# Feed-forward of a decoder layer: second products of three shared pieces behind the experts, two row and result buffers, early low parts on GpSimd

## The reference

```python
router = xf @ gate_w.T
probs = softmax(router)                        # 8 experts
top_p, top_i = top_k(probs, 2)
h = silu(xf @ expert_fc1[e].T) * (xf @ expert_fc2[e].T)       # 352 wide
out_e = h @ expert_proj[e].T                   # weighted by top_p, summed over 2 experts
s = silu(xf @ shared_fc1.T) * (xf @ shared_fc2.T)             # 1408 wide
out = x + experts + sigmoid(xf @ shared_gate_w.T) * (s @ shared_proj.T)
```

## Time and profile before

| what | us |
|---|---|
| three timed runs | 1404.07, 1404.05, 1395.89 (median 1404.05) |
| profiled execution | 1395.68 |
| its span, first to last instruction | 1393.9 |
| shared stage, from the router's first product to the last first product | 722.5 to 1085.2 |
| experts, to their last product | 1085.2 to 1354.7 |
| tail | 1354.7 to 1393.9 |

### The profile page before, as it was taken

One profiled execution on the slowest core, in us unless ns is written; L12 is line 12 of the kernel. 1 busy time (PEld: TensorE's weight loads), 2 busy tenths in 40 slices (PEclk: granted clock), 3 DMA queues, 4 the chain that ended last, 5 costly groups with the idle time before them and its releaser, 6 DMA issues. The chain is left out here.

```text
span 1393.9 us, 24148 instructions
## 1 busy us (share of the span) xinstructions
PE 1325.5 (95%) x8442; PEld 1069.3 (77%) x8442; DVE 849.8 (61%) x1516; ACT 486.1 (35%) x764; POOL 511.6 (37%) x365
## 2 busy tenths in 40 slices
PE   7999999998799999999889999999999999999995
PEld 5777778876567777777558888888878889999984
DVE  5766666787788888888644665555571242222237
ACT  4222222234366666566655111111110233323220
POOL 1122222134543434343240028421160675564055
PEclk9999999999899999999999999999999999999997
DMA  7992000003755554557200003230001434443257
GB/s 256 322 324 103 0 0 0 0 9 102 196 168 152 160 170 142 152 147 202 62 24 0 24 31 149 103 115 23 24 23 31 187 128 144 151 150 132 76 167 241
DMA packets 85035, 159.83 MB, mean 115 GB/s; under 512 B 8576, under 2 KB 61952, under 8 KB 81536
## 3 DMA queue, kind: packets, MB, share of 16 engines
q1 hardware_dynamic: 78688, 124.19, 28.4%
q0 software_dynamic: 6272, 34.61, 6.9%
HBM read 109.22 MB, written 69.47 MB: 128 GB/s over the span
## 5 line engine op out<-in xcount | busy, mean ns | idle before, releaser
L1526 ACT ACTIVATE b_pf<-b_rt,b_zero 128x1024 f32<-128x1024 f32 x128 | 142.7, 1115 | 118.6 <-PE b_rt L1197 118.2
L1366 DVE TENSOR_REDUCE b_mx<-b_rt 128x4 f32<-128x1024 f32 x128 | 156.3, 1221 | 36.0 <-PE b_rt L1185 35.4
L2064 DVE SCALAR_TENSOR_TENSOR residual<-c_yp,c_shared,residual 128x512 f32<-128x512 f32 x144 | 103.8, 744 | 114.7 <-PE c_yp L43 114.7
L41 PE MATMUL c_fc<-c_xh,c_w 128*128 128x512 f32 x352 | 137.8, 392 | 0.0
L43 PE MATMUL c_fc<-c_xh,c_w 128*128 128x512 f32 x352 | 137.2, 390 | 0.0
L42 PE MATMUL c_fc<-c_xl,c_w 128*128 128x512 f32 x352 | 137.1, 390 | 0.0
L2217 ACT ACTIVATE c_s<-c_fc 128x512 f32<-128x512 f32 x44 | 26.3, 598 | 231.8 <-PE c_fc L43 231.7
L41 PE MATMUL c_fc<-c_ring,c_xTl 128*128 x312 | 105.6, 338 | 0.0
L42 PE MATMUL c_fc<-c_ring,c_xTh 128*128 x312 | 101.1, 324 | 0.0
L43 PE MATMUL c_fc<-c_ring,c_xTh 128*128 x312 | 101.0, 324 | 0.0
L1879 POOL TENSOR_TENSOR c_w<-c_wraw,c_zero 128x1536 fp32r<-128x1536 f32 x9 | 24.7, 2749 | 202.4 <-DMA c_wraw<-in_c_ws 108.4
(11 more groups left out here) (404 smaller groups left out, 3495.1 us busy)
## 6 DMA issues: line engine op xcount, KB each, us to landing
weights_b<-b_pack SPq DMA_DIRECT2D x128, 200.0 KB
c_eraw<-in_c_we POOLq DMA_DIRECT2D x8, 2176.0 KB, 9.4
b_pack<-b_hi SPq DMA_DIRECT2D x56, 256.0 KB, 2.5
c_rows_in<-in_b_ctx SPq DMA_DIRECT2D x39, 256.0 KB, 9.6
c_rows_out<-in_b_ctx SPq DMA_DIRECT2D x39, 256.0 KB, 9.8
c_xe<-c_rows_in SPq DMA_DIRECT2D x39, 256.0 KB, 3.2
c_rows_out<-c_ye SPq DMA_DIRECT2D x39, 256.0 KB, 2.1
c_wraw<-in_c_ws SPq DMA_DIRECT2D x11, 768.0 KB, 4.2
```

Source lines behind the costliest of these rows:

```text
L41: nc.tensor.matmul(out, ll, rh, start=start, stop=False)
L1366: nc.vector.tensor_reduce(out=mx[:, :, 2 * p:2 * p + 2].rearrange("p t e -> p e t"), in_=rt[:, 0:2, :].rearrange("p e (t s) -> p e t s", s ...
L1526: nc.scalar.activation(pf[:, s:s + 2, :], rt[:, 2:4, :], ACT.Exp, scale=XD ** -0.5, bias=zero[:, :]).then_inc(e_done, 1)
L2064: nc.vector.scalar_tensor_tensor(out=X[:, t, :], in0=yp[:, (n * 4 + k) % 3, :], scalar=shared[:, t:t + 1], in1=X[:, t, :], op0=ALU.mult, o ...
```

## The change

NOW becomes 32: pieces 8, 9 and 10 are held (HELD = 3), so 12 blocks p wait for their second products, and `held_down` sums three pieces per group. The raw rows of the three pieces lie in `keep`, `wraw[2]` and `wraw[0]`, their low parts in `keep_low`, `w[2]` and `w[0]`. FIXED = 5 high parts have a place at once: four in `w[1]`, the fifth in a new tile `fifth`; the other seven reuse the five places, each behind the products that read it, and are all made in the tail. `xe` shrinks to two buffers and moves to memory that the router used, `ye` shrinks to two, `se` loses its unused columns. SP loads tile n + 4 where it loaded n + 6, and no longer waits for the shared stage's end before the first loads. ACT makes the five high parts in tiles 2 to 6; the five low parts to them are made by Pool, between its fetch and its split of expert 3. The other seven are DVE's, in a new hand-written order of the tail: there the early sums of group 3 and its late sums come before its shared sums, which finish that group, while in groups 0 to 2 the late sums do. The gate of the early gathers becomes `done + 2`.

```diff
     LAG = 2
-    NOW = STEPS - 2 * G
+    HELD = 3
+    NOW = STEPS - HELD * G
+    FIXED = 5
...
-        with ExitStack() as view:
-            xe = sb("xe", [P, 4, C], FP32, view)
...
-        se = sb("se", [P, 2, 512])
+        se = sb("se", [P, 2, 384])
         hTh, hTl = sb("hTh", [P, 2, 384], FP32R), sb("hTl", [P, 2, 384], FP32R)
-        ye = sb("ye", [P, 3, C])
+        ye = sb("ye", [P, 2, C])
+        fifth = sb("fifth", [P, C], FP32R)
+        sb("beside", [P, C // 2])
...
+        with ExitStack() as view:
+            xe = sb("xe", [P, 2, C], FP32, view)
...
         def held_raw(n):
 
-            g, second = (n - NOW) % G, (n - NOW) // G
-            return wraw[0][:, g // 2, g % 2 * C:(g % 2 + 1) * C] if second else keep[:, g, :]
+            g, f = (n - NOW) % G, n // G
+            return keep[:, g, :] if f == HID - 3 else wraw[(f + 2) % 3][:, g // 2, g % 2 * C:(g % 2 + 1) * C]
 
         def held_low(n):
-            g, second = (n - NOW) % G, (n - NOW) // G
-            return w[0][:, g // 2, g % 2 * C:(g % 2 + 1) * C] if second else keep_low[:, g, :]
+            g, f = (n - NOW) % G, n // G
+            return keep_low[:, g, :] if f == HID - 3 else w[(f + 2) % 3][:, g // 2, g % 2 * C:(g % 2 + 1) * C]
 
         def held_high(p):
 
-            if 4 <= p < 6:
-                return w[2][:, 1, C * (p - 3):C * (p - 2)]
-            return w[1][:, p % 6 // 2, p % 2 * C:(p % 2 + 1) * C]
+            u = p % FIXED
+            return fifth[:, :] if u == 4 else w[1][:, u // 2, u % 2 * C:(u % 2 + 1) * C]
 
         def pair(p):
-            return NOW + p % 2 * G + p // 2
+            return NOW + p % HELD * G + p // HELD
...
             def load(n):
-                if n >= 4:
-                    sp.wait_ge(te_done, n - 3)
-                sp.dma_start(rows_at(n), rows_in[n * P:(n + 1) * P, :]).then_inc(xe_in[n % 4], 16)
+                if n >= 2:
+                    sp.wait_ge(te_done, n - 1)
+                sp.dma_start(rows_at(n), rows_in[n * P:(n + 1) * P, :]).then_inc(xe_in[n % 2], 16)
 
             piece(2)
             for f in range(3, HID):
                 piece(f)
             sp.wait_ge(scattered, 16 * 2 * NT)
-            sp.wait_ge(ymm_done, 4 * G * 9)
-            for n in range(6):
+            for n in range(4):
                 load(n)
             for n in range(SLOTS):
                 sp.wait_ge(ye_done, n + 1)
-                sp.dma_start(rows_out[n * P:(n + 1) * P, :], ye[:, n % 3, :]).then_inc(ye_out[n % 3], 16)
-                if n + 6 < SLOTS:
-                    load(n + 6)
+                sp.dma_start(rows_out[n * P:(n + 1) * P, :], ye[:, n % 2, :]).then_inc(ye_out[n % 2], 16)
+                if n + 4 < SLOTS:
+                    load(n + 4)
...
+                if e == RING:
+                    for p in range(FIXED):
+                        pool.wait_ge(ph_done, p + 1)
+                        nc.gpsimd.tensor_tensor(held_low(pair(p)), held_raw(pair(p)), as_f32(held_high(p)), ALU.subtract).then_inc(pool_low, 1)
                 expert(e)
             done = pool.value_load(plan[0:1, E - 2:E - 1], min_val=1, max_val=SLOTS)
-            pool.wait_ge(ye_done, done + 3)
+            pool.wait_ge(ye_done, done + 2)
...
-                if 2 <= n < 8:
-                    pair_low(n - 2)
-            def expert_sum(t, k):
-                if k:
-                    dve.wait_ge(landed1[t // 4], 64)
-                    dve.wait_ge(dadded, t + 1)
+            def early_sums(a, b):
+                for t in range(a, b):
+                    dve.wait_ge(landed0[t % 3], 16 * (t // 3 + 1))
+                    nc.vector.scalar_tensor_tensor(out=X[:, t, :], in0=early[:, t, :], scalar=gain[:, 0, t:t + 1],
+                                                   in1=X[:, t, :], op0=ALU.mult, op1=ALU.add).then_inc(summed, 1)
+
+            def early_summed(t):
+                if t < POOLED:
+                    dve.wait_ge(pooled, t + 1)
                 else:
-                    dve.wait_ge(landed0[t % 3], 16 * (t // 3 + 1))
-                nc.vector.scalar_tensor_tensor(out=X[:, t, :], in0=(early, late)[k][:, t, :], scalar=gain[:, k, t:t + 1],
-                                               in1=X[:, t, :], op0=ALU.mult, op1=ALU.add).then_inc(finished if k else summed, 1)
+                    dve.wait_ge(summed, t + 1 - POOLED)
+
+            def late_sums(g):
+                for t in range(4 * g, 4 * g + 4):
+                    dve.wait_ge(landed1[g], 64)
+                    if g < G - 1:
+                        dve.wait_ge(dadded, t + 1)
+                    else:
+                        early_summed(t)
+                    nc.vector.scalar_tensor_tensor(out=X[:, t, :], in0=late[:, t, :], scalar=gain[:, 1, t:t + 1],
+                                                   in1=X[:, t, :], op0=ALU.mult, op1=ALU.add).then_inc(finished if g < G - 1 else joined, 1)
 
             def held_sums(g):
                 for k in range(4):
                     t = 4 * g + k
                     dve.wait_ge(dm_done, t + 1)
-                    if t < POOLED:
-                        dve.wait_ge(pooled, t + 1)
+                    if g < G - 1:
+                        early_summed(t)
                     else:
-                        dve.wait_ge(summed, t + 1 - POOLED)
+                        dve.wait_ge(joined, k + 1)
                     nc.vector.scalar_tensor_tensor(out=X[:, t, :], in0=sum_at(g, k), scalar=shared[:, t:t + 1],
-                                                   in1=X[:, t, :], op0=ALU.mult, op1=ALU.add).then_inc(dadded, 1)
-
-            def expert_sums(a, b, k):
-                for t in range(a, b):
-                    expert_sum(t, k)
-
-            expert_sums(POOLED, 9, 0)
+                                                   in1=X[:, t, :], op0=ALU.mult, op1=ALU.add).then_inc(dadded if g < G - 1 else finished, 1)
+
+            early_sums(POOLED, 9)
+            pair_low(5)
+            early_sums(9, 12)
+            pair_low(6)
             held_sums(0)
-            pair_low(6)
             pair_low(7)
-            expert_sums(9, 12, 0)
+            early_sums(12, 16)
+            pair_low(8)
+            late_sums(0)
             held_sums(1)
-            expert_sums(0, 4, 1)
-            expert_sums(12, 14, 0)
+            pair_low(9)
+            pair_low(10)
+            late_sums(1)
+            pair_low(11)
             held_sums(2)
-            expert_sums(4, 8, 1)
-            expert_sums(14, 16, 0)
+            late_sums(2)
+            late_sums(3)
             held_sums(3)
-            expert_sums(8, 16, 1)
...
             def pair_high(p):
                 if p == 0:
                     act.wait_ge(ymm_done, 4 * NOW)
-                if p == 6:
-                    act.wait_ge(pm_done, 1)
-                if p == 7:
-                    act.wait_ge(dm_done, 4)
+                if p >= FIXED:
+                    g, j = (p - FIXED) // HELD, (p - FIXED) % HELD
+                    if j == HELD - 1:
+                        act.wait_ge(dm_done, 4 * g + 4)
+                    else:
+                        act.wait_ge(pm_done, (HELD - 1) * g + j + 1)
                 nc.scalar.copy(held_high(p), held_raw(pair(p))).then_inc(ph_done, 1)
...
-                if 2 <= n < 8:
+                if 2 <= n < 2 + FIXED:
                     pair_high(n - 2)
-            for k in range(3):
-                act.wait_ge(ye_out[k], 16 * ((SLOTS + 2 - k) // 3))
-            act.sem_inc(ye_done, 3)
-            pair_high(6)
-            pair_high(7)
+            for k in range(2):
+                act.wait_ge(ye_out[k], 16 * ((SLOTS + 1 - k) // 2))
+            act.sem_inc(ye_done, 2)
+            for p in range(FIXED, HELD * G):
+                pair_high(p)
 
...
-                for j in range(2):
-                    p = 2 * g + j
-                    pe.wait_ge(pl_done, p + 1)
+                for j in range(HELD):
+                    p = HELD * g + j
+                    if p < FIXED:
+                        pe.wait_ge(pool_low, p + 1)
+                    else:
+                        pe.wait_ge(pl_done, p - FIXED + 1)
+                    k_w = (HID - HELD + j) % 3
                     for k in range(4):
                         a = slice(k * P, (k + 1) * P)
                         last = matmul3(nc, sum_at(g, k), (held_high(p)[:, a], held_low(pair(p))[:, a]),
-                                       (w[j][:, 0, 2 * C:PW], w[j][:, 1, 2 * C:PW]), j == 0, j == 1)
-                        if j == 1:
+                                       (w[k_w][:, 0, 2 * C:PW], w[k_w][:, 1, 2 * C:PW]), j == 0, j == HELD - 1)
+                        if j == HELD - 1:
                             last.then_inc(dm_done, 1)
-                    if j == 0:
+                    if j < HELD - 1:
                         last.then_inc(pm_done, 1)
...
```

(10 more changed lines are left out.)

7 lines of the change are left out of this document (4 added, 3 removed).

## The result

| what | before | after |
|---|---|---|
| median of 6 timed runs, us | 1402.87 (1395.89 to 1404.07) | 1384.13 (1382.6 to 1385.96) |
| profiled execution | 1395.68 | 1384.43 |
| its span | 1393.9 | 1382.6 |
| router's first product at | 722.5 | 724.7 |
| shared stage, from there to its last first product | 362.4 | 350.2 |

The changed kernel is faster by 1.3%: ratio of the timed runs 0.9873, 95% interval 0.9853 to 0.9894. The forecast was 1383.3 us. The medians are 18.7 us apart, the two profiled executions only 11.3 in span. The profile of before was taken in one of its fastest executions (1395.68, where six runs lie between 1395.89 and 1404.07), the profile of after near its median. So the stages are compared in the profiles, and the kernels by the timed runs.

The account below looks back on a forecast made before the run. PE was taken to bound the shared stage and experts, a relay of ACT, Pool and DVE the tail. 12.2 + 3.7 + 0.9 - 0.3 = 16.5 us takes 1395.68 to 1379.2; plus 4.1 gives 1383.3, range 1375 to 1394.

Parts of the forecast that it names:

- step 1: Shared stage: piece 8's 48 second products leave (10.9 us) and a long DVE low part vanishes (1.3): 12.2 us gained.
- step 2: Experts' first tiles: low parts leave DVE, five going to Pool, so none stalls beside a long Pool instruction: 3.7 us gained.
- step 3: Experts' row loads: two buffers instead of four leave 0.1 us margin in the tightest places: 0.3 us lost, at most 9.5.
- step 4: Tail behind the experts: late gathers start 4.0 us earlier, added PE and DVE work fits, DVE ends 0.9 us earlier.
- rows late: Rival, experts: three loads sent with expert weights land late, half clock behind each, 9.5 us back, 1388.7 us; chance 0.17.
- Gathers and sums in each other's way: Rival, tail: five added DVE low parts push Pool's indirect gathers, 3.7 us back, 1382.9 us (middle 1387.0); chance 0.08.
- The gain is not made: Rival, tail: it grows by what the 48 moved matmuls save, PE's groups strung out; 1391 to 1396 us; chance 0.12.
- Slower: Rival, experts: every row load comes late and stretches each tile; 1413 us at landings of 11.7 us; chance 0.05.
- a tail longer by more than 3 us: Sign of a wrong prediction: time from the experts' last product to the end grows by more than 3 us.
- PE's waits in the experts above 4 us: Sign of a wrong prediction: PE's waits in the experts exceed 4 us.

Follow-up runs that it names:

- a0: The changed kernel unaltered, measured again in the first group: median 1385.77 us, ratio 0.9901 to the kernel before.
- f3: The changed kernel unaltered, measured again in the last group: median 1387.66 us, ratio 0.9869 to the kernel before.
- f1: The changed kernel with row loads ahead of the store's wait, two early gathers in flight, no early sums on Pool: 1380.77 us, 0.9825 of the kernel before.
- f2: The changed kernel with row loads ahead of the store's wait, two early gathers in flight, one early sum on Pool: 1384.76 us, 0.9859 of the kernel before.
- b0: The changed kernel with two held pieces instead of three, all else as changed: 1396.97 us, 0.9973 of the kernel before.

## Why the prediction held, and where it missed

The forecast of 16.5 us against the profiles, term by term. The slow tiles are counted against 6.73 us, tile 37 against the 6.27 that it took before.

| term | said | measured |
|---|---|---|
| step 1, shared stage | 12.2 | 12.2 |
| step 2, low parts off the first tiles | 3.7 | 3.7 |
| step 3, late rows | -0.3 | -2.6 |
| last tiles beside the gathers | not foreseen | -1.6 |
| step 4, tail | 0.9 | 1.8 |
| all that runs ahead of the feed-forward | 0 | -2.2 |
| sum, in span | 16.5 | 11.3 |

**Step 1** was right to a tenth: 48 products at 0.227 us and the one long low part. PE was busy 266.02 of 267 us there, so what left it could shorten the stage by its full length. Taking it back alone returned 362.6.

**Step 2** was right: tiles 3 and 4 took 9.48 + 7.65 us before, 3.7 more than two usual ones, and 6.7 each after. Returning the low parts to DVE cost 3.6 at tile 3. The reason given, a low part that stands still while a long Pool instruction runs, is shown four times, by 6.43 and 4.56 us before, 6.57 with two pieces held and 4.47 with the low parts on DVE. By the rule of the Trainium skill (SBUF — State Buffer, "Who interferes with whom"), a DVE instruction with two SBUF inputs contends with a GpSimd one that reads SBUF, for a pair of ports that one of them locks; the traces agree, the DVE one ending 0.5 to 0.6 us after Pool's each time.

**Step 3** had the right mechanism and a price too small by 2.3 us. The price was read from landings of 9.6 beside 9.8 us, margin 0.1, and set at 0.3 us; the loads took 10.65 and 11.29 us and cost 0.96 and 1.68 us at tiles 11 and 16 (7.69 and 8.41 for 6.73). The error is the assumption that the landing of a transfer stays as it was when the kernel around it changes. The bound held: the prediction's 9.5 us (its 3 x 3.1 is 9.3) is far above 2.6, and no low clock followed these waits (granted clock 1.00 from 1160 to 1170 and from 1196 to 1206). The fetch after these two cost nothing: SP's load was issued 0.08 us ahead of it (1213.21 and 1213.29), not behind it. The rival *rows late* happened in two of three places, at 2.6 us instead of 9.5.

**The last tiles** were no step. The working treated the early gathers as work of Pool, hidden by PE, and gave the experts' body as full up to 1324; from 1332 on the gathers ran, and that stretch was not read for what stands beside them. In the one profile of before nothing was slow there, so the view could not have given the size; c0, the kernel before with two row buffers, shows 2.7 us at tile 36 and 5.3 at tile 37 with the old work around it. So this loss can come without the held piece and the earlier gate. It differs from kernel to kernel and from execution to execution, 0.4 to 8.8 us, and is a part of why runs of one kernel lie as far apart as they do. That the medians are further apart than the profiles fits with it, but is argued only.

**Step 4** was right and a little low. ACT's first cast came 3.2 us behind the last expert product (1348.12 against 1344.96), where before it had 4.6: the last result's copy was over at 1345.97, so its store took 2.2 us at most, and 3.6 before. The early gathers, the last of which now starts at 1336.9 and before at 1354.1, no longer run beside that store; that they are the reason is argued, not shown. DVE's list began 1.4 us earlier for it and took 0.9 longer than the 30.4 said, 0.81 of it one wait for PE; the last 0.4 are the end behind DVE, 2.5 us for 2.9. The late gathers came 3.4 us after the last expert product, for 8.7 before; PE needed 32.7 us for its 144 products, 1345.18 to 1377.9, and waited for no low part. In other executions of the changed kernel the tail took 42 to 43 us, with ACT or DVE idle for 3 to 6 us and nothing on this core to release them: the same sight as at the last tiles, now beside the late gathers. So the 1.8 us gained in the tail are those of one execution; a0 lost 3.7 us there (43.1 for 39.4) and f3 lost 2.9.

**The rivals.** *Gathers and sums in each other's way*: seen, and harmless. The late gathers took 21.2 us from the first start to the last for 19.6 before. Two of them lasted 1.62 us instead of 0.95, and each began 0.12 us ahead of a DVE low part of 0.68, in the timeline of Pool after:

```profile
1357.87 1.62 POOL L1907 DMA_INDIRECT c_late<-c_rows_out,c_rows  x1 [0.30 <-issue]
...
1367.61 1.62 POOL L1907 DMA_INDIRECT c_late<-c_rows_out,c_rows  x1 [0.30 <-issue]
```

The other low parts in that series, which began 0.18 to 0.78 us behind a gather's start or 0.35 to 0.47 ahead of it, fell beside gathers of 0.95 to 1.15 us. Sums of two SBUF inputs can do the same: in c0's timelines a gather met a series of them and ended only 0.9 us, about its own usual length, after the first sum that reads PSUM (c_fc) had begun, at 1384.16.

```profile
1380.58 4.47 POOL L1904 DMA_INDIRECT c_late<-c_rows_out,c_rows  x1 [0.30 <-issue]
```

```profile
1380.18 2.73 DVE L2159 SCALAR_TENSOR_TENSOR residual<-c_late,c_gain,residual 128x512 f32<-128x512 f32 x4
1382.83 1.40 DVE L2159 SCALAR_TENSOR_TENSOR residual<-c_early,c_gain,residual 128x512 f32<-128x512 f32 x2
1384.16 2.71 DVE L2170 SCALAR_TENSOR_TENSOR residual<-c_fc,c_shared,residual 128x512 f32<-128x512 f32 x4
```

So the rule of the Trainium skill that the prediction named holds for these gathers, and its comparison of medians (0.949 beside 0.946) could not see it; the maximum in the same rows, 1426 ns, was the hint. Of the 3.7 us only 1.6 came, and DVE waited for no late row, so the end did not move. (With the full 3.7 us the prediction's sum would be 12.8, not its 12.9.) *The gain is not made* fell: the tail shrank. *Slower* fell: 37 of 39 row loads were in time. Of the two signs of being wrong that the prediction named, one is a tail longer by more than 3 us: it shrank in this profile, though a0's grew by 3.7. The other, PE's waits in the experts above 4 us, did come: the list above sums to 5.0, and 1.7 more lie at the first transposes. It was a poor sign, since the kernel before already has 5.1 there (1.66, 1.85 and 1.61).

**The base.** The median lies 0.8 us from the forecast, but not by the forecast's sum: it had 4.1 us for the middle between two levels, and the profile missed its own figure (1379.2) by 5.2. The two errors offset each other, and that part is luck. What the profiles support is a gain of 13.5 us within the feed-forward, for 16.5 said, and in two further executions of the changed kernel 10.0 and 10.3. The timed medians give more: 18.7, 16.6 and 17.1 us in the three groups that hold the changed kernel. The profile of before, at 1395.68, lies 4 to 9 us under the four medians of its kernel (1400.01 to 1404.80), so as a base it makes every gain look smaller than the timed runs do.

## What to carry to other kernels

Where PE is busy all of a stage, the price of moved matmuls could be read to a tenth of a microsecond; the miss came from the transfers. A margin of 0.1 us between a landing and its use is not a margin: issue the load ahead of the waits that need not stand before it. Work moved into a tail is cheap only while the relay that ends it (last landing, gathers, sums) stays shorter than the engine it hides, and a helper engine ought to have nothing of its own between the last landing and the gathers.

## What the runs showed of the hardware

- Engines stand idle past the moment of their release while indirect gathers run: ACT began 4.1, 2.8 and 7.3 us behind the end of the PE work that it needed (idle 5.73, 4.43 and 9.35 us, put down to "remote" in the trace). Beside the experts this went when at most two gathers were in flight (three profiles) or none (one); beside the late gathers, which have no such limit, stalls of over 3 us came in four profiles (a0, f1, f2, f3). The profile's page has instruction transfers of a few packets in queues of their own, and it may be that these wait behind the gathers; no run separates that from other causes.
- A 256 KB load of rows sent 0.4 us behind a fetch of 2.2 MB from another queue landed with the fetch, not by its own size: 10.65 and 11.29 us beside 10.9 and 11.5, where the median of such loads was 3.2.
- An indirect gather on Pool can be lengthened by DVE work with two SBUF inputs, and it depends on a tenth of a microsecond: of 17 gathers in ten profiles that began 0.09 to 0.13 us ahead of a DVE low part, 16 took 1.60 to 1.63 us instead of 0.95, longer by that subtraction; of 13 that began 0.14 to 0.19 us ahead of one, 11 kept their 0.94 to 0.95, and the other two (1.69) also had a low part running at their start. Beside a series of sums the longest took 4.47 us (c0) and 2.48 (b0).
